# Transformer block in software pipeline: weights in quarters, late constants, and another order of the work at the end

## The chip, the cores and the metric

The program runs on one core of one Trainium2 chip. The metric is the device time of one execution in microseconds (us), median over several runs. Engines are named as the profile names them: PE is TensorE, DVE VectorE, ACT ScalarE, POOL GpSimd, SP the engine that issues most transfers.

## The reference

16 sequences of 256 tokens with 256 features go through two layers; each sequence ("batch" in the kernel) is on its own.

```python
# layer 0: attention of x on the context, 16 heads of 64, then Wo, bo, residual, layer norm
q, k, v = x @ Wq + bq, ctx @ Wk + bk, ctx @ Wv + bv          # 256 -> 1024
x = norm(softmax(mask(q k^T / 8)) v @ Wo + bo + x) * gamma + beta
# layer 1: self attention, 16 heads of 16, with an integer mask
x = norm(x + attention(x, x, mask) @ o_w + o_b)              # ln1
# cross attention on the context, 16 heads of 16, no mask
x = norm(x + attention(x, ctx) @ co_w + co_b)                # ln2
# feed forward 256 -> 1024 -> 256
x = norm(x + relu(x @ lin1_w + lin1_b) @ lin2_w + lin2_b)    # ln3
```

All data is float32.

## The kernel before

**Streams.** The work on one sequence is cut into five streams, which a software pipeline runs side by side for five successive sequences: x (transposes of input and context, first quarter of q and k), a (the attention of layer 0, called A, its Wo and ln0; also keys and values of the context for layer 1), b (self attention, B, and ln1), c (cross attention, C, and ln2's input), m (projection oc of the cross attention, ln2, feed forward, ln3, store).

**Steps.** A list of steps is written out by hand in `schedule` (L49), and every engine walks the same list and does its own part of each step. The kinds are: S, scores of a pair of heads (PE L591, then the masked copy with its extremes on DVE, L868); X, the exponentials on ACT (L698); R, the reciprocal of the sums on DVE (L879) and the scaling on POOL (L959); T, the transposes of the pair on PE (L608) with one copy each by ACT (L705) and DVE (L884); AV, the product with the values for two pairs (PE L633 or L642). J is a job: a product (PE L472) or transposes (PE L478) and its copy on DVE or ACT; h and hd are the quarters of the first feed forward product, y the second, of which a step H does the first half. LN is a layer norm's scaling on DVE (L844), N a next residual on POOL, DMA and IO are transfers issued by SP. Behind S of a pair come R of the pair before it and T of the one before that (`advance`, L105), so that the pairs form one line through all streams. A job's copy on DVE has two PSUM banks, a job's copy on ACT one.

**Bodies.** `bodies` (L320) gives the lists: four that fill the pipeline (x of 0; x, a; x, a, b; x, a, b, c), a loop of 12 turns with all five streams and 24 pairs, and four that empty it: a 15, b 14, c 13, m 12 (24 pairs), then b 15, c 14, m 13 (16 pairs), c 15, m 14 (8 pairs), and m 15. The steps of the missing streams are left out and the others keep their places in the list.

**B and C through DRAM.** Keys and queries of the 16-feature heads are split into a high and a low part on DVE (L811, L816), saved to DRAM and spread from there over the rows of `k4` and `q4`, in eight transfers each (`save_keys` L375, `spread_keys` L386, `spread_queries` L397). The values of C come back from DRAM as well (`load_values` L366). All of these stand on SP's queue in the order of the list, with their waits before them.

**The start.** SP loads x, the context and Wq, the mask, Wk, Wv (1 MB each, L414), the integer mask, Wo, layer 1's attention weights, the small vectors (L428 to L446) and the feed forward weights. ACT loads bq, bk and bv as columns (L656) under one semaphore, and ACT and DVE wait for all three (L659, L746). At the end of the first body ACT waits for all small vectors (L730), DVE too, and adds three bias rows and makes the integer mask (L748); POOL waits for both ahead of its first step (L911, L912).

Of the kernel before, what the change touches and what calls it, by code (L numbers as in the profile page):

```python
# [16 lines left out]
P = 128  # L17
BATCH, TOK, D = 16, 256, 256
TT, DT = TOK // P, D // P
HEADS = 16  # L20
# [27 lines left out]

def schedule(present, carried):  # L49

# [12 lines left out]
    def emit(items):  # L63
        steps.extend(x for x in items if x[3] in present)
# [35 lines left out]
    emit(head)  # L100
    line = [p[1:] for p in carried]
    ready = len(line)
    waiting = [("AV", name, p // 2 - 1, stream) for name, p, stream in line[:1]]

    def advance(g, jobs):  # L105

        nonlocal waiting
        if max(0, ready - 1) <= g - 1 < len(line):
            steps.append(("R",) + line[g - 1])
        emit(jobs)  # L110
        if 0 <= g - 2 < len(line):
            steps.append(("T",) + line[g - 2])
        if ready <= g < len(line):
            steps.append(("X",) + line[g])
        steps.extend(waiting)
        waiting = []
        if 0 <= g - 2 < len(line):
            name, p, stream = line[g - 2]
            if p % 2:
                waiting = [("AV", name, p // 2, stream)]  # L120

    g = ready
    for i, o in enumerate(order):
        if STREAM[o[0]] in present:
            line.append(step("S", *o)[1:])
            steps.append(step("S", *o))
            advance(g, after[o])
            g += 1
        elif carried and "a" not in present and i < 3:
            advance(g, after[o])  # L130
            if i < 2:
                g += 1
            else:
                line, ready, g = [], 0, 0
        else:
            emit(after[o])
    if not closed:
        for k in range(g, g + 3):
            advance(k, [])
        emit(wo + os + first)  # L140
# [3 lines left out]
class Body:  # L144
# [3 lines left out]
    def __init__(self, x, a, b, c, m, before=None, base=None):  # L148
        self.batches = {"x": x, "a": a, "b": b, "c": c, "m": m}
        self.before = before  # L150
        self.base = base or (before.end if before else (0, 0))
        self.present = {s for s, n in self.batches.items() if n is not None}
# [3 lines left out]
        self.steps = schedule(self.present, carried)  # L156
# [7 lines left out]
    def slot(self, step, ring):  # L164

        _, name, p, stream = step
        if stream == STREAM[name]:
            return (self.base[0] + self.pairs.index(("S", name, p, stream))) % ring
        return (self.base[0] - len(self.before.pairs) + self.before.pairs.index(("S", name, p, STREAM[name]))) % ring

    def earlier(self, step, back, same):
# [10 lines left out]
        if len(self.present) == 5:  # L182
# [799 lines left out]
```

## Time and profile before

| | us |
|---|---|
| median of three runs | 2088.13 (2084.88 to 2092.41) |
| profiled execution | 2080.84 |
| its span, first to last instruction | 2079.1 |
| PE busy in the span | 1893.7 (91%) |
| DVE, ACT, POOL busy | 1326.9, 1196.1, 984.2 |
| mean granted clock of PE | 0.970 of full |

Matmuls overlap, so PE's busy time is the time in which at least one was under way. A matmul step's cost is read best from start to start. The granted clock of a stretch is a mean over its two levels.

### The profile page before, as it was taken

To read this page: it belongs to the slowest core of one execution; us is meant where nothing else is said; L and a number is where in the kernel's file an instruction comes from. 1 tells how busy PE (TensorE), PEld (TensorE's weight loads), DVE (VectorE), ACT (ScalarE), POOL (GpSimd) and SP (SyncE) were. 2 spreads that over 40 slices of the span, in tenths; PEclk is the share of its full clock that TensorE was granted. 3 is DMA by queue.
4 is the path that set the end of the run, shared out by engine and by line. 5 is a ranking of instruction groups with operands and counts; after the bars stand their busy time and mean duration, and the time that the engine had idled before them with its cause. 6 is when DMAs were issued, how large, how long until landed. Compare 5 with 4: busy or idle time off the path is not lost.

```text
span 2079.1 us, 42825 instructions
## 1 busy us (share of the span) xinstructions
PE 1893.7 (91%) x12608; PEld 1451.6 (70%) x12608; DVE 1326.9 (64%) x5194; ACT 1196.1 (58%) x3985; POOL 984.2 (47%) x1014
## 2 busy tenths in 40 slices
PE   3999999999999999999899999999999999986776
PEld 2776777777776777777677777767777777764554
DVE  1465676766767676666767666676766667664642
ACT  1454766556565665656666565666656566663632
POOL 0233555536364553645455464544546464552622
PEclk8999999999999999999999999999999999998988
DMA  7032525171422517143260714326071422507120
GB/s 209 28 61 58 87 64 82 33 118 33 77 43 59 92 33 118 33 73 46 54 97 33 119 32 72 47 54 97 32 118 33 80 39 64 86 21 117 25 42 6
DMA packets 145109, 135.94 MB, mean 65 GB/s; under 512 B 23280, under 2 KB 139760, under 8 KB 144880
## 3 DMA queue, kind: packets, MB, share of 16 engines
q1 hardware_dynamic: 141760, 132.97, 35.6%
q8 instruction: 132, 2.16, 0.5%
q14 instruction: 97, 0.79, 0.2%
q10 hardware_dynamic: 3120, 0.01, 0.1%
HBM read 90.99 MB, written 41.94 MB: 64 GB/s over the span
## 4 chain that ended last, share of the span: by engine, by line
PE 64%; issue 16%; POOL 8%; DVE 7%; SPq 2%; ACT 1%; DMA 1%; POOLq 0%; DVEq 0%; ACTq 0%
PE ps_gd L472 27%; PE ps_t L608 10%; PE ps_ga L472 9%; PE ps_s L591 9%; POOL prob L959 7%; PE ps_av L633 5%; PE ps_av L642 4%; DVE prob L868 2%; PE ps_ga L478 1%; DVE res_ln L826 1%; DVE res_ln L844 1%; DVE stats_ln L829 1%; POOL res_ln L947 1%; ACT k_ctx L685 1%; POOL rstd_ln L924 1%
## 5 line engine op out<-in xcount | busy, mean ns | idle before, releaser
L959 POOL TENSOR_TENSOR prob<-prob,recip 128x512 f32<-128x512 f32 x768 | 788.9, 1048 | 927.3 <-DVE recip L879 926.1
L698 ACT ACTIVATE prob<-prob,ext 128x256 f32<-128x256 f32 x1536 | 757.9, 501 | 23.4 <-DVE ext L868 23.3
L705 ACT ACTIVATE prob_t<-ps_t 128x512 f32<-128x512 f32 x384 | 229.2, 597 | 462.5 <-PE ps_t L608 462.4
L608 PE MATMUL ps_t<-ident,prob 128*128 128x128 f32 x3072 | 416.5, 277 | 38.1 <-POOL prob L959 22.7
L608 PEld LDWEIGHTS ps_t<-ident,prob 128*128 128x128 f32 x3072 | 357.4, 142 | 92.6 <-POOL prob L959 31.8
L884 DVE COPY prob_t<-ps_t 128x512 f32<-128x512 f32 x384 | 262.5, 684 | 174.7 <-PE ps_t L608 170.5
L698 ACT ACTIVATION_READ_ACCUMULATOR prob<-prob,ext 128x1 f32 x1536 | 296.9, 193 | 0.0
L868 DVE CUSTOM_DVE_ANT_0 prob<-ps_s,mask_a 128x256 f32<-128x256 f32 x512 | 186.7, 421 | 111.3 <-PE ps_s L591 108.2
L868 DVE CUSTOM_DVE_ANT_0 prob<-ps_s,mask_b 128x256 f32<-128x256 f32 x512 | 187.5, 419 | 73.9 <-PE ps_s L591 73.8
L868 DVE CUSTOM_DVE_ANT_0 prob<-ps_s,zero 128x256 f32<-128x256 f32 x512 | 185.7, 419 | 34.9 <-PE ps_s L591 34.7
L591 PE MATMUL ps_s<-k_ctx,q 64*128 64x256 f32 x1024 | 150.4, 413 | 24.8 <-DVE ext L868 16.2
L685 ACT ACTIVATE k_ctx<-ps_ga,col_bk 128x256 f32<-128x256 f32 x128 | 53.8, 471 | 157.2 <-PE ps_ga L472 140.4
L591 PEld LDWEIGHTS ps_s<-k_ctx,q 64*128 64x128 f32 x1024 | 91.3, 190 | 69.0 <-issue 56.0
L472 PE MATMUL ps_gd<-x_t,wq 128*128 128x256 f32 x512 | 126.6, 391 | 10.2 <-DVE x_t L775 10.2
L472 PE MATMUL ps_ga<-c_t,wk 128*128 128x256 f32 x512 | 127.4, 392 | 0.0
L868 DVE DVE_READ_ACCUMULATOR2_ANT ext<- 128x1 f32 x1536 | 126.9, 83 | 0.0
L633 PE MATMUL ps_av<-prob_t,v 128*64 128x256 f32 x1024 | 124.6, 385 | 0.8 <-DVE prob_t L884 0.8
L472 PE MATMUL ps_gd<-wv,c_t 128*128 128x256 f32 x512 | 124.5, 386 | 0.0
L472 PE MATMUL ps_gd<-wl,h_t 128*128 128x256 f32 x512 | 119.8, 388 | 3.7 <-issue 3.7
L826 DVE TENSOR_TENSOR res_ln<-ps_gd,res_ln 128x512 f32<-128x512 f32 x64 | 44.3, 692 | 122.9 <-PE ps_gd L472 122.9
L844 DVE TENSOR_SCALAR res_ln<-res_ln,mv_ln,rstd_ln 128x256 f32<-128x256 f32 x128 | 82.8, 689 | 62.5 <-issue 54.3
L472 PE MATMUL ps_gd<-wo,k_ctx 128*128 128x256 f32 x512 | 117.2, 382 | 1.0 <-issue 1.0
(87 smaller groups left out, 2567.4 us busy)
## 6 DMA issues: line engine op xcount, KB each, us to landing
k_B<-k_parts_B SPq DMA_DIRECT2D x128, 128.0 KB, 5.2
q_B<-q_parts_B SPq DMA_DIRECT2D x128, 128.0 KB, 9.7
k_C<-k_parts_C SPq DMA_DIRECT2D x128, 128.0 KB, 4.4
q_C<-q_parts_C SPq DMA_DIRECT2D x128, 128.0 KB, 4.8
k_parts_C<-k_hl SPq DMA_DIRECT2D x16, 512.0 KB, 3.0
k_parts_B<-k_hl SPq DMA_DIRECT2D x16, 512.0 KB, 3.4
q_parts_B<-q_hl SPq DMA_DIRECT2D x32, 256.0 KB, 2.4
q_parts_C<-q_hl SPq DMA_DIRECT2D x32, 256.0 KB, 11.5
```

Source lines behind the costliest of these rows:

```text
L472: last = nc.tensor.matmul(out, lhs[i], rhs[i], start=i == 0, stop=i == n - 1)
L591: last = nc.tensor.matmul(two(ps_s[e])[:, t, :], q[r, t * P:(t + 1) * P], k[r], start=True, stop=True)
L608: last = nc.tensor.transpose(two(ps_t[e])[:, kt, qt * P:(qt + 1) * P], src[:, e, qt, kt * P:(kt + 1) * P], ident[:, :])
L633: last = nc.tensor.matmul(two(ps_av)[e * DH0:(e + 1) * DH0, j, :], v0[:, kt, h * DH0:(h + 1) * DH0], pt[:, e, kt, :], start=kt == 0, stop= ...
L642: last = nc.tensor.matmul(ps_av[j * SLOT:(j + 1) * SLOT, 0:TOK], v1[s][:, kt, c:c + SLOT], pt[:, e, kt, :], start=kt == 0, stop=kt == TT - ...
L685: last = nc.scalar.activation(out[:, c, :], ps[:, m, :], ACT.Relu if name == "h" else ACT.Identity, bias=bias[:, c:c + 1])
L698: last = nc.scalar.activation(tile, tile, ACT.Exp, bias=ext[:, slot, e, t:t + 1], scale=-1.0, accum_out=sums[:, slot, e, t:t + 1])
L705: nc.scalar.activation(prob_t[:, body.slot(step, PT_RING), 0], two(ps_t[0]), ACT.Copy).then_inc(pt_act[s], 1)
L844: last = nc.vector.tensor_scalar(y[:, t, :], y[:, t, :], mv[ln][:, t, 0:1], rstd[ln][:, t:t + 1], ALU.subtract, ALU.mult)
L868: last = nc.vector.tensor_tensor_reduce(out=prob[:, slot, e, t, :], in0=two(ps_s[e])[:, t, :], in1=mask, scale=-SCALE[s], scalar=BIG, op0= ...
L884: nc.vector.tensor_copy(prob_t[:, body.slot(step, PT_RING), 1], two(ps_t[1])).then_inc(pt_dve[s], 1)
L959: nc.gpsimd.tensor_tensor(rows, rows, recip[:, slot, e].unsqueeze(2) .to_broadcast([P, TT, TOK]), ALU.mult).then_inc(normed[s], 1)
```

## The change

At the start each of Wq, Wk and Wv is loaded in four pieces of 256 columns, all first quarters ahead of all second ones, each with a semaphore of its own; the row of bo moves up behind the first quarters. ACT and DVE wait for bq and bk alone, and ACT for bv at the first weighed values. The waits for the small vectors, with the bias rows and the integer mask, move from the end of the first body to the end of the second on ACT, DVE and POOL.

At the end the four bodies that empty the pipeline become one, with a list of its own. Sequences 13, 14 and 15 appear in it under the stream names c, c2, c3 and m2, m3, m4. Its 48 pairs come in the order A of 15, B of 14, C of 13, B of 15, C of 14, C of 15; C of 15 uses the buffers `k4`, `q4` and `v1` of B. The three feed forwards stand between the pairs. Before, the first 24 of these pairs were interleaved. The lists of the filling bodies and of the loop have the same steps as before.

```diff
+LAST = {"a": 1, "b": 2, "b2": 1, "c": 3, "c2": 2, "c3": 1, "m": 4, "m2": 3, "m3": 2, "m4": 1}
+HOME = {"c3": "B"}
...
+def last_schedule(carried):
+    steps += [dma("c", "k", "C"), ln("c", "ln1"), job("b", "x1T"), job("a", "mask")]
+    places = [
+        ("A", "a", [
+            [job("b", "ks"), dma("b", "save", "B"), job("a", "k", 1)],
+            [job("b", "qs"), dma("b", "q", "B"), job("a", "q", 1), job("c", "x2T")],
+            [job("c", "qc"), dma("c", "q", "C"), job("a", "v", 0)],
+            [job("a", "k", 2), job("a", "q", 2), io("c", "value_c")],
+            [job("m", "oc"), job("b", "vs")],
+            [ln("m", "ln2"), job("a", "k", 3), job("a", "q", 3)],
+            [job("m", "x3T"), job("a", "v", 1), job("a", "v", 2), res("m", "res3", 0)],
+            [job("a", "v", 3), res("m", "res3", 1)]]),
+        ("B", "b", [
+            [job("m", "h", 0), res("c", "res2", 0)],
+            [job("m", "h", 1), res("c", "res2", 1)],
+            [job("a", "kc"), res("b", "res1", 0)],
+            [half("a", "wo"), res("b", "res1", 1), res("a", "res0", 0)],
+            [job("a", "wo"), job("a", "vc"), io("a", "save_c")],
+            [ln("a", "ln0"), job("m", "hd")],
+            [job("b2", "x1T"), job("m", "h", 2)],
+            [job("b2", "ks"), dma("b2", "save", "B"), job("b2", "qs"), dma("b2", "q", "B")]]),
+        ("C", "c", [
+            [],
+            [half("m", "y")],
+            [job("m", "y")],
+            [job("b", "os"), job("b2", "vs")],
+            [ln("c2", "ln1"), ln("m", "ln3"), io("m", "store")],
+            [job("c2", "x2T")],
+            [job("c2", "qc")],
+            [dma("c2", "k", "C"), dma("c2", "q", "C")]]),
+        ("B", "b2", [
+            [],
+            [],
+            [],
+            [job("m2", "oc"), io("c2", "value_c")],
+            [ln("m2", "ln2")],
+            [job("m2", "x3T"), res("m2", "res3", 0)],
+            [res("m2", "res3", 1)],
+            [dma("c3", "k", "C"), res("c2", "res2", 0)]]),
+        ("C", "c2", [
+            [res("c2", "res2", 1)],
+            [job("m2", "hd"), res("b2", "res1", 0)],
+            [res("b2", "res1", 1)],
+            [job("b2", "os")],
+            [ln("c3", "ln1"), job("m2", "h", 0)],
+            [job("c3", "x2T")],
+            [job("c3", "qc"), dma("c3", "q", "C"), io("c3", "value_c")],
+            [job("m2", "h", 1)]]),
+        ("C", "c3", [
+            [],
+            [],
+            [ln("m2", "ln3"), io("m2", "store")],
+            [job("m3", "oc")],
+            [ln("m3", "ln2")],
+            [job("m3", "x3T"), res("m3", "res3", 0)],
+            [job("m3", "h", 0), res("m3", "res3", 1)],
+            [job("m3", "h", 1), res("c3", "res2", 0)]])]
+    for name, stream, jobs in places:
+        for p in range(PAIRS):
+            if stream == "c3" and p == 0:
+                steps += [job("m2", "h", 2), half("m2", "y"), job("m2", "y")]
+            steps.append(("S", name, p, stream))
+            line.pairs.append(steps[-1][1:])
+            line.advance(g, jobs[p])
+            g += 1
+    line.advance(g, [job("m3", "h", 2), res("c3", "res2", 1)])
+    line.advance(g + 1, [job("m3", "hd")])
+    line.advance(g + 2, [])
+    steps += [job("m4", "oc"), half("m3", "y"), ln("m4", "ln2"), job("m3", "y"), job("m4", "x3T"), ln("m3", "ln3"),
+              io("m3", "store"), job("m4", "h", 0), job("m4", "hd"), res("m4", "res3", 0), res("m4", "res3", 1),
+              job("m4", "h", 1), job("m4", "h", 2), half("m4", "y"), job("m4", "y"), ln("m4", "ln3"), io("m4", "store")]
...
-            body = Body(BATCH - 1, BATCH - 2, BATCH - 3, BATCH - 4, BATCH - 5,
-                        Body(BATCH - 2, BATCH - 3, BATCH - 4, BATCH - 5, None), body.end)
-            for n in range(4):
-                body = Body(*[None] * (n + 1), *range(BATCH - 1, BATCH - 5 + n, -1), body)
-                yield body
+            late = Body({"x": BATCH - 1, "a": BATCH - 2, "b": BATCH - 3, "c": BATCH - 4})
+            yield Body({s: BATCH - n for s, n in LAST.items()}, late, body.end)
...
-            def spread_keys(s, b):
+            def spread_keys(s, b, home):
                 sp.wait_ge(k_saved[s], count(b, 16, 16))
-                if s == "C" and not (isinstance(b, int) and b == 0):
+                if s != home:
+                    sp.wait_ge(scored["B"], count(b, HEADS, HEADS))
+                elif s == "C" and not (isinstance(b, int) and b == 0):
                     sp.wait_ge(scored["C"], count(b - 1, HEADS, HEADS))
...
-            for w, n in ((wq0, "q0"), (wk0, "k0"), (wv0, "v0")):
-                sp.dma_start(w[:, :, :], wide(L0 + "W" + n[0])).then_inc(w_in[n], 16)
-                if n == "q0":
-                    sp.dma_start(mask_u8[:, :, :], m_d[:, 0]).then_inc(m_in, 16)
+            for i in range(4):
+                cols = slice(i * D, (i + 1) * D)
+                for w, n in ((wq0, "q"), (wk0, "k"), (wv0, "v")):
+                    sp.dma_start(w[:, :, cols], wide(L0 + "W" + n)[:, :, cols]).then_inc(w_in0[n][i], 16)
+                    if i == 0 and n == "q":
+                        sp.dma_start(mask_u8[:, :, :], m_d[:, 0]).then_inc(m_in, 16)
+                if i == 0:
+                    sp.dma_start(row["bo0"][:, :], io[L0 + "bo"].partition_broadcast(P)).then_inc(w_in["bo0"], 16)
...
-                        pe.wait_ge(w_in[name + "0"], 16)
+                        pe.wait_ge(w_in0[name][i], 16)
...
-                              ).then_inc(w_in["bias0"], 16)
-            act.wait_ge(w_in["bias0"], 48)
+                              ).then_inc(w_in["bias_v" if n == "bv" else "bias0"], 16)
+            act.wait_ge(w_in["bias0"], 32)
...
-            dve.wait_ge(w_in["bias0"], 48)
+            dve.wait_ge(w_in["bias0"], 32)
...
-                if body.before is None and body.batches["x"] is not None:
+                if body.present == {"x", "a"}:
                     constants_of_layer1()
...
-            pool.wait_ge(w_in["small"], 16 * small)
-            pool.wait_ge(dve_const, 2)
+            pool.wait_ge(w_in["bo0"], 16)
+            pool.wait_ge(dve_const, 1)
...
+                if body.present == {"x", "a"}:
+                    pool.wait_ge(w_in["small"], 16 * small)
+                    pool.wait_ge(dve_const, 2)
```

## Rows read from the trace of the kernel before

**Rows 1.** Stretches of single bodies (us, busy of PE, PEld, DVE, ACT, POOL, PEclk, DMA, GB/s)

```profile
1515.05:1633.48 118.43, 115.04 (x788) 89.03 (x788) 81.11 (x321) 72.75 (x243) 60.33 (x62) 1.00 0.36 65
1753.59:1874.36 120.77, 113.63 (x767) 86.88 (x765) 81.70 (x322) 73.77 (x248) 61.99 (x64) 0.97 0.37 61
1874.36:1970.82 96.46, 68.07 (x447) 48.80 (x445) 54.08 (x218) 48.38 (x162) 42.96 (x45) 0.86 0.44 66
1970.82:2034.75 63.93, 44.12 (x249) 31.04 (x249) 30.62 (x118) 27.53 (x91) 23.45 (x27) 0.84 0.27 43
2034.75:2079.10 44.35, 26.92 (x124) 19.61 (x124) 9.15 (x22) 5.62 (x13) 7.24 (x9) 0.79 0.02 6
```

**Rows 2.** Timeline of the start, all engines (start us, duration, instruction, idle before it)

```profile
16.21 0.69 DVE L775 COPY x_t<-ps_gd 128x512 f32<-128x512 f32 x1 [14.46 <-DMA col_bv<-L_xattn_bv]
...
25.77 1.98 PE L591 MATMUL ps_s<-k_ctx,q 64*128 64x256 f32 x8 [2.36 <-ACT k_ctx L685]
...
27.68 2.79 PE L472 MATMUL ps_ga<-c_t,wk 128*128 128x256 f32 x8
...
42.44 1.09 DVE L751 TENSOR_TENSOR row_b<-row_b,h_t 128x256 f32<-128x256 f32 x3 [20.95 <-DMA h_t<-L_xattn_lin_b]
...
45.98 2.08 PE L591 MATMUL ps_s<-k_ctx,q 64*128 64x256 f32 x8 [15.51 <-DVE ext L868]
```

**Rows 3.** DMA issues of the first 60 us (KB each, us from issue to landing)

```profile
col_bk<-L_xattn_bk ACTq DMA_DIRECT2D x1, 4.0 KB, 8.5
col_bv<-L_xattn_bv ACTq DMA_DIRECT2D x1, 4.0 KB, 14.2
```

**Rows 4.** Timeline of PE in the last body with A pairs

```profile
1825.06 1.13 PE L591 MATMUL ps_s<-k_ctx,q 64*128 64x256 f32 x8
1826.12 3.72 PE L472 MATMUL ps_gd<-wl,h_t 128*128 128x256 f32 x16
1829.68 1.04 PE L608 MATMUL ps_t<-ident,prob 128*128 128x128 f32 x8
1830.64 0.50 PE L591 MATMUL ps_s<-k_C,q_C 64*128 64x256 f32 x4
```

**Rows 5.** A group of the page's costliest (busy, mean ns of one, idle before)

```profile
L698 ACT ACTIVATE prob<-prob,ext 128x256 f32<-128x256 f32 x1536 | 757.9, 501 | 23.4 <-DVE ext L868 23.3
```

**Rows 6.** Timeline of DVE at a batch's last layer norm

```profile
2014.40 1.44 DVE L844 TENSOR_SCALAR res_ln<-res_ln,mv_ln,rstd_ln 128x256 f32<-128x256 f32 x2
```

**Rows 7.** Three stretches with few jobs, columns as in group 1

```profile
1858.47:1874.36 15.89, 13.13 (x90) 8.61 (x89) 12.15 (x52) 10.57 (x38) 8.89 (x10) 0.79 0.15 28
1920.88:1966.44 45.56, 35.88 (x270) 24.19 (x270) 31.36 (x134) 32.88 (x115) 30.46 (x30) 0.91 0.02 7
2011.02:2034.75 23.73, 15.03 (x106) 9.58 (x105) 18.91 (x77) 15.83 (x54) 12.38 (x14) 0.78 0.04 12
```

**Rows 8.** Timeline of PE, scores of pairs in three light slots

```profile
1942.82 0.80 PE L591 MATMUL ps_s<-k_B,q_B 64*128 64x256 f32 x4 [0.29 <-DVE ext L868]
...
1947.75 0.50 PE L591 MATMUL ps_s<-k_B,q_B 64*128 64x256 f32 x4
...
1953.70 0.51 PE L591 MATMUL ps_s<-k_B,q_B 64*128 64x256 f32 x4
```

**Rows 9.** Timeline of PE, y of batches 14 and 15

```profile
2002.29 8.80 PE L472 MATMUL ps_gd<-wl,h_t 128*128 128x256 f32 x32 [2.69 <-issue]
...
2064.25 7.14 PE L472 MATMUL ps_gd<-wl,h_t 128*128 128x256 f32 x32 [0.98 <-issue]
```

**Rows 10.** Timeline of PE and SP, products and first scores of B and C

```profile
1877.73 1.97 PE L472 MATMUL ps_gd<-x_t,w_k 128*128 128x256 f32 x8 [2.77 <-ACT x_t L677]
...
1904.67 0.80 PE L591 MATMUL ps_s<-k_B,q_B 64*128 64x256 f32 x4 [11.08 <-issue]
...
1978.66 1.29 SPq L400 DMA_DIRECT2D q_parts_C<-q_hl  x2
...
1993.67 0.50 PE L591 MATMUL ps_s<-k_C,q_C 64*128 64x256 f32 x4
```

More of the change, by code:

```diff
@@ L46, with __init__, advance @@
 NEXT = {"a": "b", "b": "c", "c": "m"}
+LAST = {"a": 1, "b": 2, "b2": 1, "c": 3, "c2": 2, "c3": 1, "m": 4, "m2": 3, "m3": 2, "m4": 1}
+HOME = {"c3": "B"}
+class Line:
+    def __init__(self, steps, carried):
+        self.steps = steps
+        self.pairs = [p[1:] for p in carried]
+        self.ready = len(self.pairs)
+        self.waiting = [("AV", name, p // 2 - 1, stream) for name, p, stream in self.pairs[:1]]
+    def advance(self, g, jobs):
+        pairs = self.pairs
+        if max(0, self.ready - 1) <= g - 1 < len(pairs):
+            self.steps.append(("R",) + pairs[g - 1])
+        self.steps.extend(jobs)
+        if 0 <= g - 2 < len(pairs):
+            self.steps.append(("T",) + pairs[g - 2])
+        if self.ready <= g < len(pairs):
+            self.steps.append(("X",) + pairs[g])
+        self.steps.extend(self.waiting)
+        self.waiting = []
+        if 0 <= g - 2 < len(pairs):
+            name, p, stream = pairs[g - 2]
+            if p % 2:
+                self.waiting = [("AV", name, p // 2, stream)]
 def schedule(present, carried):
@@ L61, in schedule, with here @@
     steps = []
-    def emit(items):
-        steps.extend(x for x in items if x[3] in present)
+    def here(items):
+        return [x for x in items if x[3] in present]
     order = [(name, 2 * q + j) for name, q in
@@ L98, in schedule @@
     }
[L100 to L120, printed above, removed]
@@ L122, in schedule @@
-    g = ready
-    for i, o in enumerate(order):
+    steps += here(head)
+    line = Line(steps, carried)
+    g = line.ready
+    for o in order:
         if STREAM[o[0]] in present:
-            line.append(step("S", *o)[1:])
             steps.append(step("S", *o))
-            advance(g, after[o])
+            line.pairs.append(steps[-1][1:])
+            line.advance(g, here(after[o]))
             g += 1
[L129 to L134, printed above, removed]
@@ L248, in program @@
         two = lambda t: t[:, :].rearrange("p (a n) -> p a n", a=2)
-        w_in = {n: sem("w_in_" + n) for n in ("q0", "k0", "v0", "bias0", "out0", "attn1", "mlp", "small", "mask")}
+        w_in = {n: sem("w_in_" + n) for n in ("bias0", "bias_v", "bo0", "out0", "attn1", "mlp", "small", "mask")}
+        w_in0 = {n: [sem(f"w_in_{n}0_{i}") for i in range(4)] for n in "qkv"}
         x_in, c_in, m_in = sem("x_in"), sem("c_in"), sem("m_in")
@@ L259, in program @@
         att = "ABC"
-        small = len(col) - 3 + 2 + len(row) + 3
+        small = len(col) - 3 + 2 + len(row) - 1 + 3
         SPREAD = 8
@@ L340, in load @@
                 b = body.batch(step)
-                if body.batches["a"] is None:
+                if "a" not in body.present:
                     return
@@ L712, in evac_weighed @@
                     act.wait_ge(weighed[s], count(b, QUADS, quad + 1))
+                    if isinstance(b, int) and b == 0:
+                        act.wait_ge(w_in["bias_v"], 16)
                     for j in range(2):
@@ L901, in _ @@
                      "AV": evac_weighed}.get(step[0], lambda *_: None)(body, step)
-                if body.before is None and body.batches["x"] is not None:
+                if body.present == {"x", "a"}:
                     constants_of_layer1()
```

63 lines of the change are left out of this document (40 added, 23 removed).

## The prediction

> **What bounds the kernel now.** I read the page first (busy shares and the 40 slices), then the stretches of single bodies, then the timeline of the first 60 us and of the last 325. In the loop TensorE sets the pace: a body of 118.4 us has it busy 115.0 us at full granted clock [rows 1]. The change leaves the loop's order as it is, so the question is the two ends. In the last body that has A pairs TensorE is still busy 113.6 of 120.8 us; in the three stretches behind it it is busy 68.1 of 96.5, 44.1 of 63.9 and 26.9 of 44.4 us, and the granted clock is 0.86, 0.84 and 0.79 [rows 1]. Together this end takes 120.8 + 96.5 + 63.9 + 44.4 = 325.5 us. In them TensorE idles 72.8 us and runs slow on top. At the start the first tile is copied by VectorE only at 16.21, first scores stand ready at 25.77, and then nothing moves until VectorE adds the bias rows at 42.44; the second scores run at 45.98 [rows 2].
>
> **The head, part by part.** (1) VectorE and ScalarE no longer wait for the column of bv. Its row says 14.2 us to landing, bk's 8.5 [rows 3]; bv landed at 16.2, so was issued at 2.0, and bk just ahead of it, which puts bk at 10 at the latest. It may come sooner, since less is queued in long packets; nothing before 4, when x_tok's transposes start, could use it, and their results are complete at about 7 (an estimate: c_tok comes next on the same queue). I take 8.5 for the first copy, between the bounds 7 and 10. (2) Wq, Wk, Wv come in 12 pieces with the first pieces in front. From first copy to first scores the kernel needs 25.77 - 16.21 = 9.6 us [rows 2] and this stays: 18.1. The later quarters have to be there about one pair apart; all 4 MB of weights up to Wo and more land well before 42 today, so I cost them nothing. If this cover fails, the product of k's quarter 1, which is the next on TensorE, waits. (3) The long wait goes: ScalarE, VectorE and GpSimd wait for the small constants after body 1, which today ends at 107.7 and then at some 85, still over 40 us behind the landing. What is late next is TensorE's own k product: the second scores follow the first by a 2.0 us score step and the 2.8 us product that today hides in the wait [rows 2], so at 22.9, against 45.98: 23.1 gained. (4) The bias sums and the mask, 1.4 us from 42.44 on VectorE, move behind body 1, where body 2's first scores wait for them: 1.4 back. [...] With no 16 us hole before it I give 1 us for that and the q product behind it. (6) Nine more DMAs on SP's queue, each around 0.5 us of issue, push all later loads by 5 us, which nothing waits for. Bounds of these: 19 to 26; taken 22.7, say **23 us**.
>
> **The end.** Nothing is removed: the same 48 pairs and jobs stand in another order, so I price slots. A slot is what lies between two score steps. On TensorE the steps cost, start to start, 1.06 (A's scores), 0.44 (B's and C's, 0.50 long), 0.97 (turning a pair), 1.8 (a product of eight matmuls: half of 3.56), 3.56 (half of y or wo), 1.0 (weighing B or C) and 1.9 (A) [rows 4]. ScalarE needs 4 exponentials of 0.50 us and a copy [rows 5], 2.6, VectorE four reductions, two reciprocals and a copy, some 2.3, GpSimd two products, some 2.1. A layer norm adds 1.44 on VectorE [rows 6]; for the last one of a batch, which multiplies and adds a row behind it, I count 3.6, two more passes. A slot's price is its largest engine's sum. For the last A body this rule gives 120.5, where 120.8 were measured [rows 1]. For slots with few jobs it falls short: 13.3 against 15.9, 40.6 against 45.6 and 19.6 against 23.7 [rows 7], 16% in sum, since a pair's chain and a clock of 0.78 to 0.91 come in. Two empty slots take 5.95 us together [rows 8], where ScalarE has some 5.7.
> The new order, step by step:
> - 20 full slots (all of A, of B of batch 14, the first four of C of 13), 6.7 us for a slot with two products, less towards the end: 112 by the rule, plus 3 because x1T and h2, and h after h, now share one bank of ScalarE with nothing but a turn between. 115.
> - 26 light slots (C 13's last four, B 15, seven of C 14, seven of C 15), 99.2 by the rule, 3.8 each, since residuals, norms and projections are spread over them; times 1.16: 115.
> - The slot of C 14's last pair, which holds h1, h2 and all of y: 12.2, and 2.7 for the wait before y that the same series had at 2002.29 [rows 9]: 15.
> - From C 15's last scores to the turn of its pair 6: 3.4 today, with h1 and h2 in it 6.
> - The rest, 44.4 us today. Batch 14's hd and y (8.9 us of TensorE) now fill the waits around the last projection, where TensorE has only 26.9 us of work in 44.4 [rows 1]. By steps: turn, weigh, hd, turn, weigh 7.2 with two short waits; oc 1.8; y 7.1; x3T and its copy 1.8; h0, hd, h1 5.3; h2 with a wait 2.8; a wait of 1 and y 7.1, and from y's end to the end 2079.1 - 2071.4 = 7.7 [rows 9]: 42.
> Sum 293, against 325.5: **32 us** gained. Round trips through DRAM: for B of 15 TensorE stood idle for 11.1 us until 1904.67, 27 us after its key product began [rows 10]. Now the product stands over 30 us ahead of its first score, behind C's eight pairs: hidden. For C of 15 the save starts at 1978.66 and the scores ran at 1993.67 [rows 10], so 15.0 us are enough; the new order has 17 us of TensorE work between. It is the tightest one. C 14's keys can only be spread after C 13's last scores, with eight B pairs, 27 us, for it. If they fail, the exposed part adds in full.
> SP's queue stays in order: the store of batch 12 waits for its norm ahead of C 14's spread, but that waits for C 13's last scores anyway, some 10 us later.
> **Sum:** 23 + 32 = 55. The span goes from 2079.1 to 2024 and the profiled execution (2080.84, below all three timed runs) to 2026. The median shown is 7.3 higher, 2088.13, and I put the gain on that: 2033. What measurement can tell from no change is about 0.3%, 6 us.
>
> **Rivals.**
> R1, the pairs' own pace. The light slots run as the rule says or as the empty ones do, 2.98 [rows 8], because jobs fill the clock's holes: 99 instead of 115, and the drain two better. For: a clock of 1.00 where TensorE is kept busy [rows 1]. Against: all three light stretches were 12 to 21% above the rule. With a head of 25, gain 75: 2013.
> R2, low clock at the end. [...] At the lower level a slot without jobs took 4.9, from 1942.82 to 1947.75 [rows 8]. If half of the 26 slots do so, 13 times 1.2 is 16 us, and with a head of 20 the gain is 36: 2052. Against: small products stand in most slots.
> [...]
> R3, the quarters come late. Loads of 1 KB rows in place of 4 KB ones bind the first pairs, and the first A attention runs at the pace of the transfers: half the head's gain, 11, is lost: 2044. Against: bv's column, queued beside x, c and over a megabyte of weights, was in at 16.2 [rows 3], and the 12 pieces are wanted over more than 30 us, k's second at 20.
> R4, slower: the round trips open up. In the new order three attentions wait on a spread (B 15, C 14, C 15) with no pair of another kind behind them in the hand-written order. If SP's in-order queue held each as B 15 was held today, 27 us from the key product [rows 10], and the pairs between did not cover it, 81 us would be added: 2033 + 81 = 2114. It decides when the uncovered part is over 18 us for each. Against: eight pairs, at least 24 us, stand ahead of each.
> R5, the change does not bite, as bk or a late constant still holds the start and the end's slots lose what they gain: under 6 us either way.
>
> **Numbers.** Forecast 0.60, R1 0.12, R2 0.18, R3 0.06, R4 0.02, R5 0.02. Faster takes the first four, 0.96; same 0.01 and slower 0.03 share the rest. The range goes to R1 and R2: 2013 to 2053.
>
> **What would show it.** First copy by VectorE at 7 to 10; second scores at 22 to 24; no engine waiting for a bias row; second body's start near 86. The part behind the loop near 293 us, TensorE's idle time in it 35 to 45 instead of 73, no idle over 3 us before a first score of B 15, C 14 or C 15, and the last product ending 7.7 before the end. Wrong would be: a wait on Wk's quarter before 30, any spread that shows as idle time, granted clock under 0.85 in the light stretch, or light slots of over 4.8 us.

## The result and the profile after

The changed kernel takes 2005.18 us in the median of four runs (2000.32 to 2012.25), the kernel before 2086.51 beside it on the same chip (2083.13 to 2092.41): a ratio of 0.961, 95% interval 0.9573 to 0.9647. The forecast was 2033, with 2013 to 2053. The sign was right and the size was not: 81 us were gained where 55 were forecast, and the range's lower bound lies 8 us above the result. The profiled execution took 2005.85 us, its span is 2004.1, against 2079.1. Two executions further down, one of `head_only` (2101.76 us) and one of `h2_moved` (6322.16 us), ran in a slower state and are left out of the medians and ratios given there.

First the stretches of the changed kernel, columns as in [rows 1]. In order: one loop body; the end in five parts (20 full slots, 19 light slots, the slot of C 14's last pair with h1, h2 and y, 7 light slots, the rest); the whole end; the loop.

```profile
1486.85:1606.59 119.74, 116.58 (x788) 90.05 (x788) 81.24 (x321) 72.67 (x243) 60.27 (x62) 0.99 0.37 63
1730.01:1845.26 115.25, 109.62 (x714) 85.73 (x712) 74.24 (x284) 64.01 (x213) 54.66 (x58) 0.99 0.54 85
1845.26:1914.66 69.40, 56.71 (x449) 39.50 (x448) 57.82 (x241) 54.95 (x188) 48.50 (x49) 0.93 0.41 62
1914.66:1928.30 13.64, 12.37 (x64) 10.11 (x60) 3.47 (x14) 5.24 (x19) 2.07 (x3) 1.00 0.86 136
1928.30:1956.81 28.51, 22.20 (x169) 15.19 (x168) 23.90 (x94) 18.91 (x64) 16.57 (x18) 0.88 0.03 10
1956.81:2004.10 47.29, 34.91 (x196) 28.27 (x192) 16.77 (x46) 10.70 (x31) 13.96 (x17) 0.95 0.04 12
1730.01:2004.10 274.09, 235.81 (x1582) 178.81 (x1580) 176.21 (x678) 153.81 (x511) 135.77 (x142) 0.95 0.38 61
270.51:1730.01 1459.50, 1394.44 (x9459) 1077.96 (x9457) 992.97 (x3889) 894.07 (x2989) 738.17 (x757) 0.99 0.37 65
```

The end fell from 325.5 to 274.1 us. TensorE idles 274.09 - 235.81 = 38.3 us in it, before 72.8 [rows 1]; the other 17 us of the gain are busy time, for the most part the same matmuls at a higher clock, 0.95 in the mean where the last three stretches before had 0.79 to 0.86. This is a split of the time and not yet the price of the clock: in `filled_light2` below the light slots have a clock of 0.98 and 1.00 in place of 0.93 and 0.88 and take 97.2 us for 97.9. `filled_old_end` measures the price in the old end.

Two things in reading such rows. Busy time of TensorE is less than the sum of its matmuls: in the kernel before the 512 with Wo take 382 ns each in the mean, 195.6 us together, and are counted as 117.2 us busy. Steps overlap too: the first three of [rows 4] take 1.13 + 3.72 + 1.04 = 5.89 us, and from the start of the first to the start of the fourth it is 5.58. And in all fourteen traces the record of the granted clock has two values, 1.00 and 0.50, the lower one most often for 3.41 us at a time (15 of the changed kernel's 17 pieces); 0.93 or 0.88 is a mean over both.

Next the start, on the timeline, to be read against [rows 2], and the landings of bk and bv against [rows 3].

```profile
6.86 0.69 DVE L880 COPY x_t<-ps_gd 128x512 f32<-128x512 f32 x1 [5.11 <-DMA col_bk<-L_xattn_bk]
...
7.65 3.75 PE L574 MATMUL ps_gd<-x_t,wq 128*128 128x256 f32 x8 [1.20 <-DVE x_t L880]
...
14.04 1.28 ACT L788 ACT_TABLE_LOAD   x1 [14.04 <-PE ps_ga L574]
...
16.32 2.08 PE L694 MATMUL ps_s<-k_ctx,q 64*128 64x256 f32 x8 [2.37 <-ACT k_ctx L788]
18.33 2.69 PE L574 MATMUL ps_ga<-c_t,wk 128*128 128x256 f32 x8
...
20.95 1.13 PE L694 MATMUL ps_s<-k_ctx,q 64*128 64x256 f32 x8
```

```profile
col_bk<-L_xattn_bk ACTq DMA_DIRECT2D x1, 4.0 KB, 5.5
col_bv<-L_xattn_bv ACTq DMA_DIRECT2D x1, 4.0 KB, 8.2
```

The 16 us hole in front of the second scores is gone: they run at 20.95 in place of 45.98. Bodies are counted from 0 here, as the prediction does: body 0 has x of sequence 0 alone, body 1 the first attention A, body 2 the first B. What the prediction and the expectations call the second body is body 2. It starts at 81.88, before at 108.64. Seven of the traces here have this same start, and body 2 starts in them at 79.6 to 82.2; in the earliest, `mixed_first`, the granted clock up to there was 1.00, here 0.98. What a single edit of the start gives can be told only above these 2.5 us. The rest of the start is a chain without a gap to spare: bk's landing, the copies, q's product (3.75 us for eight matmuls that take 1.99 at 22.02), k's (2.76), and ScalarE's table load of 1.28 ahead of the first keys. The changed kernel's stretches of q's product, the first and the second scores:

```profile
7.65:11.40 3.75, 3.75 (x9) 3.03 (x10) 0.50 (x1) 0.00 (x0) 0.00 (x0) 1.00 1.12 328
16.32:18.40 2.08, 2.08 (x9) 1.38 (x9) 0.00 (x0) 0.00 (x0) 0.00 (x0) 0.51 1.10 350
20.95:22.08 1.13, 1.13 (x10) 0.75 (x9) 0.00 (x0) 1.02 (x3) 0.00 (x0) 1.00 1.13 302
```

The same scores take 2.08 us at 0.51 and 1.13 at 1.00. For q's product no low clock is shown: the record begins at 12.9 us, and stretches ahead of that read 1.00. That it ran at the lower level is an estimate, from its 3.75 us against 1.99.

Span against span: 26.8 us from the start, 51.4 from the end, and 3.2 given back in the loop, whose code is the same: 75.0. The median moved by 81.3, because the profiled execution before (2080.84) was lower than all the runs beside it.

What TensorE waited for in the end, as groups of waits (us in total, times, longest). The changed kernel:

```profile
PE ps_t L711 <- POOL prob L1064: 5.2, 10, 1.1
PE ps_s L694 <- DVE ext L973: 4.1, 7, 0.9
PE ps_t L711 <- DVE prob_t L989: 3.5, 4, 1.6
...
PE ps_ga L580 <- DVE res_ln L949: 3.3, 3, 1.7
PE ps_ga L574 <- ACT x_t L780: 3.2, 2, 2.0
```

And the old end, from the first experiment below, where it stands behind the new start:

```profile
PE ps_s L724 <- issue: 12.6, 2, 10.4
PE ps_t L741 <- POOL prob L1094: 10.0, 18, 1.8
PE ps_s L724 <- DVE ext L1003: 9.9, 13, 1.9
PE ps_ga L610 <- DVE res_ln L979: 7.7, 2, 3.8
PE ps_gd L604 <- ACT x_t L810: 7.2, 5, 2.8
```

The round trip of B 15 (the 10.4 us before its first scores, put down to "issue" since nothing in the profile releases it) has no row any more, and the waits on a pair's own chain (its scaling on GpSimd, its extremes and copies on VectorE) and on the jobs' copies are about halved.

### The profile page after: what moved, and what is told of

It reads as the page before. It is cut to its first block, busy times and chain, and to the rows that moved or that the text cites. A ratio compares the mean times of both kernels' runs of the same rounds, so it can differ in the third digit from the quotient of the medians.

```text
span 2004.1 us, 42839 instructions
## 1 busy us (share of the span) xinstructions
PE 1876.5 (94%) x12608; PEld 1443.8 (72%) x12608; DVE 1327.3 (66%) x5194; ACT 1194.2 (60%) x3985; POOL 984.2 (49%) x1014
## 4 chain that ended last, share of the span: by engine, by line
PE 64%; issue 18%; POOL 9%; DVE 5%; ACT 2%; DMA 0%; POOLq 0%; DVEq 0%; ACTq 0%
PE ps_gd L574 27%; PE ps_t L711 10%; PE ps_ga L574 9%; PE ps_s L694 9%; POOL prob L1064 7%; PE ps_av L736 5%; PE ps_av L745 4%; DVE prob L973 2%; PE ps_ga L580 1%; DVE res_ln L931 1%; POOL res_ln L1052 1%; ACT k_ctx L788 1%; DVE stats_ln L934 1%; DVE res_ln L949 1%; ACT prob L801 0%
## 5 line engine op out<-in xcount | busy, mean ns | idle before, releaser
L949 DVE TENSOR_SCALAR res_ln<-res_ln,mv_ln,rstd_ln 128x256 f32<-128x256 f32 x128 | 84.4, 701 | 63.3 <-issue 56.7
L574 PE MATMUL ps_gd<-wo,k_ctx 128*128 128x256 f32 x512 | 117.2, 382 | 1.7 <-issue 1.0
```

The lines of the kernel that those rows point to most:

```text
L574: last = nc.tensor.matmul(out, lhs[i], rhs[i], start=i == 0, stop=i == n - 1)
L949: last = nc.vector.tensor_scalar(y[:, t, :], y[:, t, :], mv[ln][:, t, 0:1], rstd[ln][:, t:t + 1], ALU.subtract, ALU.mult)
```

## The experiments

Twelve kernels ran, in three groups, each beside the kernel before (2085.14, 2086.44 and 2085.0 us in the median). Where no interval is given there was one run. Of the edits only the lines that matter are shown.

**The two halves apart.** `head_only` has the new start and the four old emptying bodies:

```
-            late = Body({"x": BATCH - 1, "a": BATCH - 2, "b": BATCH - 3, "c": BATCH - 4})
-            yield Body({s: BATCH - n for s, n in LAST.items()}, late, body.end)
+            late = Body({"x": BATCH - 2, "a": BATCH - 3, "b": BATCH - 4, "c": BATCH - 5})
+            body = Body(dict(zip("xabcm", range(BATCH - 1, BATCH - 6, -1))), late, body.end)
+            for n in range(4):
+                body = Body(dict(zip("abcm"[n:], range(BATCH - 1, BATCH - 5 + n, -1))), body)
+                yield body
```

> The changed start with the four emptying bodies of before. If the two ends are independent: second body's first TensorE work at 82 us as in the changed kernel (108.7 before), part behind the loop 325 us as before, time 27 us under before, a ratio of 0.987. Rival, that the loop or the end gives part of it back: ratio over 0.990, with the part behind the loop or a loop body longer than before.

2059.59 us, ratio 0.986 (0.9822 to 0.9898). Body 2 starts at 82.16. The part behind the loop takes 324.2 us, as four bodies (columns as above):

```profile
1734.04:1853.74 119.70, 112.28 (x766) 86.06 (x765) 81.72 (x322) 73.77 (x248) 61.58 (x64) 0.99 0.37 60
1853.74:1951.29 97.55, 68.39 (x446) 48.74 (x445) 54.09 (x218) 48.48 (x162) 43.37 (x45) 0.86 0.44 66
1951.29:2015.44 64.15, 44.28 (x248) 31.05 (x248) 30.63 (x118) 27.53 (x91) 23.61 (x27) 0.84 0.28 43
2015.44:2058.22 42.78, 25.31 (x124) 18.50 (x124) 9.15 (x22) 5.62 (x13) 7.26 (x9) 0.84 0.02 7
```

`end_only` is the reverse: weights whole, all three biases waited for, constants in the first body, and the new end.

> The start of before with the new single body at the end. If the end's gain is its own: part behind the loop 274 us, 51 less than before, ratio 0.975, and the two parts add up to the whole change within 5 us. Rival, that the end is helped by the earlier start (transfers, clock): part behind the loop over 280.

2036.63 us, ratio 0.9764 (0.9737 to 0.9791). The part behind the loop takes 274.5 us, body 2 starts at 109.14. The halves are independent: in the traces the new start alone brings body 2 forward by 26.5 us and the new end alone is 51.0 shorter, against 26.8 and 51.4 together. The medians give 25.6 + 48.5 = 74 us of the 81, within what medians of a few runs tell.

**Is it the clock?** The light slots fell short of the forecast's price, and the clock in them was 0.93 and 0.88, not 0.78 to 0.91. `filled_light2` is the changed kernel with transposes of the identity wherever TensorE waits in the light slots; they write to PSUM that is overwritten right after:

```
+                    if light:
+                        busy(body, step, two(ps_t[e])[:, 0, 0:P], 2)
+                    pe.wait_ge(normed[s], count(b, HEADS, 2 * p + e + 1))
```

> The changed kernel with extra transposes of the identity, whose results are overwritten, where TensorE waits in the light slots: 2 ahead of each half of a turn, 4 to 14 ahead of oc and the transposes of x2 and x3. The output stays the same. If the low clock after a wait is what the light slots still lose: granted clock 0.93 and 0.88 there go to about 1.00 and the 26 light slots from 97.9 to about 91 us. Rival, that VectorE, ScalarE and GpSimd set them: clock up, time the same or longer by up to 5 us, as the extra work stands in the way.

2004.86 us, ratio 0.9611 (0.9585 to 0.9638): no change. Its two light stretches:

```profile
1843.58:1913.60 70.02, 64.41 (x543) 47.58 (x542) 58.90 (x242) 55.12 (x190) 48.50 (x49) 0.98 0.42 64
1927.24:1954.38 27.14, 24.59 (x217) 18.19 (x216) 23.81 (x94) 19.17 (x66) 17.04 (x19) 1.00 0.03 10
```

The clock is at 0.98 and 1.00 now, and the slots take 97.2 us against 97.9. The added transposes could have cost as much as the clock gave, so a comparison without them counts more: six traces have the changed kernel's end as it is. In the changed kernel TensorE had the low clock for 17.1 us of the light slots and they took 97.9 us, in the five others (`end_only`, `warm_head`, `whole_weights`, `bv_waited`, `const_early`) for 13.7 us and they took 98.4. In the full slots, where TensorE is busy 95%, it does count: `const_early` had no low clock there and took 113.6 us, the others 3.4 us of it and 115.2. `filled_old_end` asks the same of the old end: `head_only` with such transposes in the three bodies without an A, 70 of them in front of B 15's first scores.

> The new start with the old end (four bodies that empty in turn), and identity transposes on TensorE where its steps wait in the three emptying bodies without a last-layer A, 70 of them ahead of B15's first scores, so that the engine hardly rests there. Theory (the low clock made an own part of the old end's time, so whole attentions win partly by keeping the clock): the part behind the loop falls from 324 to 305-312 us, about 2045. Rival (the gaps are waits for other engines and for the round trip, the low clock lies inside them): 322-328 us, the time stays at 2060 +/- 4.

2054.09 us, ratio 0.9845 (0.9823 to 0.9868), the part behind the loop 321.5 us:

```profile
1732.44:1856.16 123.72, 116.15 (x770) 88.59 (x769) 82.20 (x324) 74.24 (x249) 61.93 (x64) 0.96 0.35 59
1856.16:1954.07 97.91, 86.94 (x660) 70.03 (x659) 54.29 (x217) 48.22 (x162) 43.27 (x45) 0.97 0.43 66
1954.07:2013.06 58.99, 49.46 (x344) 38.27 (x342) 30.53 (x117) 27.01 (x91) 23.23 (x26) 0.94 0.29 46
2013.06:2053.95 40.89, 28.95 (x190) 23.46 (x190) 9.15 (x22) 5.83 (x14) 7.25 (x9) 0.95 0.02 7
```

The clock rises from 0.84 to 0.94 and 0.95, and the three filled bodies lose 97.55 + 64.15 + 42.78 - 97.91 - 58.99 - 40.89 = 6.7 us; the first, where nothing was changed, was 4.0 longer this time. So of the 51 us of the new end some 7 can be the clock, or more if the added transposes stood in the way themselves, which was not measured. The run fell short of its theory (305 to 312 us). The first of the three, the one with the round trip, gained nothing from it.

**Is it the whole attentions, or only one body without drains?** `mixed_first` keeps one body, but its first 24 pairs stand interleaved as in the loop (AAABCBACBBCC by twos), and only B 15, C 14 and C 15 follow as whole attentions:

```
+    order = [(name, 2 * q + j) for name, q in
+             zip("AAABCBACBBCC", (0, 1, 2, 0, 0, 1, 3, 1, 2, 3, 2, 3)) for j in range(2)]
```

> One body at the end as in the change, but its first 24 pairs interleaved A, B, C as before, with Wo's layer norm late; B 15, C 14, C 15 then follow. If doing A as a whole first is what hides the round trip of B 15 through DRAM: TensorE idles 12 to 20 us ahead of B 15's first scores and the part behind the loop takes 288 to 297 us. Rival, that having one body with no drain between is the gain: that part stays within 5 us of 274.

2009.27 us, ratio 0.9633 (0.9606 to 0.966), the part behind the loop 278.4. The first 24 pairs and B 15's first scores:

```profile
1727.91:1864.59 136.68, 116.19 (x796) 90.28 (x794) 86.95 (x334) 76.87 (x258) 63.23 (x66) 0.96 0.47 76
```

```profile
1864.59 0.80 PE L695 MATMUL ps_s<-k_B,q_B 64*128 64x256 f32 x4 [13.68 <-issue]
```

The interleaved order does its 24 pairs in 136.7 - 13.7 = 123.0 us, the changed kernel in 1863.17 - 1730.01 = 133.2. It saves 10, some 2 of them because the transposes of x2 and the product qc of C 14 stand behind B 15's first scores in it, and pays 14 for B 15's round trip, which now has nothing in front of it. So whole attentions among the first 24 pairs bring 4 of the 51 us, by covering that one trip; the other 47 come with the single body. It has two parts, a line of pairs that doesn't run dry between the streams, and norms, projections and feed forwards placed between other pairs; no run tells them apart.

**The head's three parts.** One is undone in each of the next three. `whole_weights`, each weight in one transfer:

```
-            for i in range(4):
+            for i in range(1):
```

> The changed kernel with each first-layer weight loaded by one transfer again, the rest of the new start kept. Theory (the quarters bring the small constants and the first weight forward, part of the head's gain): the first copy on ScalarE at 8 to 9 in place of 6.86, the first scores at 17.5 to 19 in place of 16.32, 1 to 3 us of the 27. Rival (the first projections wait for whatever lands last anyway): first scores within 0.5 of 16.32.

2005.08 us. The first copy waits for bk until 8.69, the first scores run at 17.21; but k's product takes 1.89 us, above 2.76, and the first scores 1.14 at a granted clock of 1.00, above 2.08 at 0.51; the second scores run at 20.20 and body 2 starts at 81.03. The first scores, 0.9 later, fall between theory and rival. A start 1.8 us later is given back within five steps: nothing is left. `bv_waited`, on ScalarE and VectorE alike:

```
-            act.wait_ge(w_in["bias0"], 32)
+            act.wait_ge(w_in["bias0"], 48)
```

> The changed kernel, but ScalarE and VectorE wait for the value bias together with the two other biases before their first step, as the kernel before does. Theory: the first copy waits for the third bias, at 10 to 14, and the first scores come 3 to 7 us later than 16.32. Rival (with the quarters the value bias lands close behind the others): first scores at most 1.5 us later.

2010.01 us. First copy at 10.34, first scores at 18.75, 2.4 later, but body 2 at 82.57, 0.7 later. Of the 4.2 us by which its span is longer 2.7 lie in the loop and 0.4 in the end, which this edit does not touch. The copy came as the theory had it, the first scores between theory (3 to 7 later) and rival (at most 1.5); for body 2 it is under 1 us, less than the same start varies by. `const_early`, on all three engines:

```
-                if body.present == {"x", "a"}:
+                if body.present == {"x"}:
```

> The changed kernel with the late constants back in the first body. Theory (they hold ScalarE and VectorE ahead of the second scores, the largest term of the head): second scores at 40 to 47 in place of 20.95, body 2 18 to 24 us later than 81.88, about 2025. Rival (body 1 has slack that takes the delay up): body 2 under 10 us later.

2039.7 us, body 2 at 111.48, 29.6 later, above the 18 to 24 expected. Its timeline, VectorE's bias rows and TensorE's second scores:

```profile
44.44 1.10 DVE L856 TENSOR_TENSOR row_b<-row_b,h_t 128x256 f32<-128x256 f32 x3 [32.31 <-DMA h_t<-L_xattn_lin_b]
```

```profile
47.98 2.08 PE L694 MATMUL ps_s<-k_ctx,q 64*128 64x256 f32 x8 [26.80 <-DVE ext L973]
```

This is the whole head, and more: with twelve weight pieces ahead of them on SP's queue the constants land 2 us later than before (44.44 against 42.44 in [rows 2]). The late constants are worth 29.6 us, the quarters and the bias of v nothing that can be told; without the late constants the new start would have lost 2 to 3 (111.48 against 109.14 in `end_only`).

**What is left at three places.** `warm_head` puts identity transposes on TensorE at the very start, behind the context's transposes and behind k's first product, and has ScalarE load its table by a small activation at the beginning.

> The changed kernel with identity transposes on TensorE before and between the first steps, and ScalarE's table loaded by a small activation at the very start. Theory (the first projections run at the low or just raised clock and the 1.28 us table load stands in the chain from the keys to the first scores): first scores at 12.5-14 in place of 16.32, body 2 some 3 us earlier, 2002. Rival (the chain is set by landings and by the copies on ScalarE and VectorE): first scores 15.5-16.5, 2005.

2000.5 us, ratio 0.9602 (0.9574 to 0.963). TensorE's first steps:

```profile
1.43 1.97 PE L754 MATMUL ps_av<-ident 128*128 128x128 f32 x8 [1.43 <-POOL ident L1024]
...
8.08 1.97 PE L575 MATMUL ps_gd<-x_t,wq 128*128 128x256 f32 x8 [0.54 <-DVE x_t L890]
...
12.86 1.13 PE L695 MATMUL ps_s<-k_ctx,q 64*128 64x256 f32 x8 [0.43 <-ACT k_ctx L798]
```

First scores at 12.86, body 2 at 76.79, 5.1 earlier. Here the matmuls' own pace does count: q's and k's products take 1.97 and 1.89 us in place of 3.75 and 2.76, and the first scores 1.13 at a granted clock of 1.00 in place of 2.08 at 0.51. The table load left the chain too: from the end of k's product to the first scores it is 1.1 us, before 2.4, so it is 1.3 of the 3.5 us at the first scores. The 5.1 are the best case: against the changed start at its luckiest (79.6) it is 2.9, and in `tuned`, with the same start as here, body 2 came at 80.0.

`h2_moved` takes h2 from the slot of B 14's pair 6, where it waits for ScalarE's copy of x1T (the idle time in this row of the changed kernel), and puts it into that of C 13's pair 0:

```profile
1815.10 3.68 PE L574 MATMUL ps_ga<-x_t,wl 128*128 128x256 f32 x8 [2.03 <-ACT x_t L780]
```

```
-            [job("b2", "x1T"), job("m", "h", 2)],
+            [job("b2", "x1T")],
```

> The changed kernel with the h2 step of c1 put one slot block later (from the slot of B6's last pair, where x1T of b2 uses the same bank, to C0's). Theory (slot B6 took 8.67 us against 4.81 by the rule since h2 waits 2.03 us for ScalarE's copy of x1T): B6 falls to about 5, C0 grows by under 1, 3 us gained, 2002. Rival (the slots share what the engines owe, as in the light stretch as a whole, 97.9 against 99.2): the stretch of light slots keeps 97-99 us and the time 2005 +/- 2.

1997.02 us, ratio 0.9594 (0.9558 to 0.963), the part behind the loop 270.7. The slots from B's pair 6 to C's pair 3, first the changed kernel, then this one:

```profile
1811.91:1845.26 33.35, 30.13 (x197) 23.33 (x196) 22.25 (x88) 17.32 (x60) 14.89 (x18) 0.95 0.62 96
```

```profile
1806.46:1835.70 29.24, 28.23 (x197) 22.25 (x196) 22.08 (x88) 17.32 (x60) 14.89 (x18) 1.00 0.73 109
```

4.1 us, 1.9 of them matmuls at a higher clock: in this execution a wait of 2 us cost nearly as much again through the clock of the product behind it (3.68 us at 0.54, 1.99 at 1.00 in `h2_moved`). It need not: in `const_early`, behind the same wait of 2.03 us, that product took 1.99 us at 1.00.

`split_ln3` gives the last norm's scaling, gain and bias slots of their own. In the changed kernel they keep VectorE in one piece, while a pair's transposed probabilities wait for their copy:

```profile
1847.61 2.87 DVE L949 TENSOR_SCALAR res_ln<-res_ln,mv_ln,rstd_ln 128x256 f32<-128x256 f32 x4
1850.51 0.69 DVE L956 TENSOR_TENSOR res_ln<-res_ln,row_g 128x512 f32<-128x512 f32 x1
1851.23 0.69 DVE L958 TENSOR_TENSOR res_ln<-res_ln,row_b 128x512 f32<-128x512 f32 x1
1851.84 0.68 DVE L989 COPY prob_t<-ps_t 128x512 f32<-128x512 f32 x1
```

> The changed kernel with the last layer norm's VectorE work (3.6 us in one piece) as three steps in slots of their own. Theory (one long piece on VectorE holds back the copies of the transposed probabilities: C5 and C6 take 6.28 and 6.86 us against 3.62 and 4.58): those slots fall, 3 to 5 us gained, about 2001. Rival (a slot before took less than its rule, so the stretch is bound by the sums of the engines' work and not by its pieces): light slots 97-99 us as before, 2005 +/- 2.

1999.93 us, ratio 0.9587 (0.9567 to 0.9607), the part behind the loop 270.8. Its light stretches:

```profile
1845.19:1913.88 68.69, 56.09 (x449) 38.43 (x448) 58.64 (x241) 55.09 (x188) 49.61 (x49) 0.93 0.41 62
1927.52:1953.48 25.96, 19.17 (x169) 13.23 (x168) 23.62 (x94) 18.92 (x64) 17.46 (x18) 1.00 0.03 11
```

94.65 us against 97.91, with VectorE as busy as before (82.3 against 81.7 us). Of the 3.3 us 0.7 lie in the first stretch and 2.6 in the second. Filling the waits gave nothing in these slots, cutting up what is waited for did. In the slot shown the edit also takes apart two norms that stood together (the scaling x4 is of both), so there the cutting isn't told from the moving; in the second stretch the norm stood alone.

`tuned` has these three edits together.

> The changed kernel with the three edits that each gave something: identity transposes and the table load at the start (body 2 came 5.1 us earlier), h2 out of slot B6 (the part behind the loop 3.4 us shorter), the last norm in three pieces (3.3 us shorter). Theory (they touch different places and add): body 2 at 77, the part behind the loop 266 to 269, 1990 to 1996 us. Rival (h2 moved and the split norm relieve the same VectorE queue): the part behind the loop 270 to 272, 1998.

2000.58 us in five runs (1997.05 to 2003.72), ratio 0.9588 (0.9564 to 0.9612), above the 1990 to 1996 expected. The end adds up as expected, 266.7 us, 7.4 shorter; body 2 came at 80.00, not 77, since q's product took 3.75 us again in this execution; and the loop took 3.5 us more. By spans it is 5.3 us below the changed kernel, by ratios 0.9588 against 0.961 with intervals that overlap, and it is level with each single edit. Faster than the kernel before it surely is; than the changed one probably, by some 0.2%.

## Why the prediction fell short, step by step

**Bounds now** was right: the loop is TensorE's (busy 1394.4 of 1459.5 us), the change acts at both ends only, and these add up.

**Head, (1).** bk was taken to allow the first copy at 8.5, between 7 and 10. It was 6.86, below the lower bound, and 8.69 with the weights whole: the quarters, which the sum priced at nothing, bring bk forward. First scores 16.32 for 18.1.

**(2)** right: no product waits for a quarter. **(3)** right, and the largest term: second scores at 20.95 for 22.9, the difference being (1). **(4)** was given 1.4 us and cost nothing: no engine was late behind body 1. Body 2 follows after the same 0.9 us as in every kernel here with either place of the constants (80.95 to 81.88; 110.55 to 111.48 in `const_early`), and from its start to the loop it is 188.6 us, before too. **The 1 us for the second scores and the q product behind them**: no run shows this term. From the second to the third scores the kernel before takes 5.66 us (45.98 to 51.64), the changed one 3.84 (20.95 to 24.79), 1.8 less. The second scores take 2.08 us at a granted clock of 0.50 before and 1.13 at 1.00 now, the q product 2.88 and 1.99. The head gave 26.8 against 22.7, over its upper bound of 26 (26.5 to 29.0 over the seven traces with this start). The reasoning that the constants carry it was right; `whole_weights` and `bv_waited` show that the other two parts, on which (1) and (2) rest, are worth next to nothing on their own: of a start 1.8 or 3.5 us later all or most was given back, in one trace each, k's product taking 1.89 us in both in place of 2.76 and the first scores 1.14 and 1.13 at a granted clock of 1.00 in place of 2.08 at 0.51.

**End.** Of the five terms three stand to within 2 us: the 20 full slots 115.25 for 115, the slot with y 13.6 for 15 (the wait before y was 1.2, not 2.7), and C 15's last scores with the rest 47.3 for 48. The term that failed is the second: **26 light slots, 99.2 by the rule, times 1.16: 115**. They took 69.40 + 28.51 = 97.9. The bare rule was right in sum, and this is R1's price for them, which had 0.12.

The factor came from three stretches of before [rows 7] and was carried to slots that are not of their kind. In `head_only` nine slots of C 14 and B 15, seven of them empty and two with a norm, took 33.65 us where the rule has about 28, a fifth more; in `filled_old_end`, at a clock of 0.95 for 0.85, the same nine took 31.24. So there are two parts: the clock, and the pair's own chain, 5.95 us for two empty slots [rows 8], where the rule has some 5.4. In the new order the list gives only six of the 26 nothing beside their pair; they took 18.06 us for the rule's 16 to 17. The other twenty carry a norm, a residual or a product and took 79.9 for 82 to 83, less than the rule. There a slot's largest engine is VectorE with a norm or GpSimd with a residual, and their excess lies partly beside the next slot's TensorE work: a largest sum for each slot counts it in full. A factor on top went the wrong way. That both parts were at work in the nine slots is shown; why the twenty stay under the rule is only argued.

**R1** was nearest in time (2013) and right for the light slots; its gain of 75 is the gain of the span, 75.0, though part of that is luck: the head gave 2 and the rest of the end 1 more than it had, and the loop took 3. Its reason, that jobs fill the clock's holes, was not right: filling the holes altogether (`filled_light2`) changed nothing. **R2** had 0.18. Taken together the light slots of the changed kernel are not bound by the clock; in the old end its own share is some 7 us. The clock does fall in the light slots of the changed kernel, to 0.93 and 0.88 against 0.99 in the full ones. A low clock had a price at the start (2.08 us for the first scores at 0.51, 1.13 at 1.00 in `warm_head`) and in the slot of h2 (3.68 us for the product at 0.54, 1.99 at 1.00). In the light slots it came to nothing: TensorE is busy 56.7 of 69.4 us and 22.2 of 28.5 there and waits for another engine anyway. **R3** did not come: with the weights whole body 1 takes 62.9 us from its first scores, in quarters 64.6, the clock being 1.00 and 0.97, and no product waits for a piece. **R4** did not come either: the changed kernel shows no wait over 3 us before any attention's first scores; but its mechanism is real, 13.7 us for B 15 in `mixed_first`, where its cover is gone. **R5** is out.

**Numbers.** Of the 28 us between 2033 and 2005, 4 are the head and 19 the end (17 of them light slots), and the loop took 3 back. The other 8 are the median on which the gain was put: it lay 7.3 us over the profiled execution before, and after the two agree within 0.7. So the forecast failed by the factor 1.16, and the range by its base: its lower bound was R1, which has the light slots right and the gain of 75 that the span shows. The 8 us by which the result lies under that bound are this base.

## What to carry to other kernels

Price a reordered stretch by each slot's largest engine, and correct it only with slots that carry the same mix of jobs: an excess measured on empty slots belongs to the chain of an empty slot (here a fifth in nine nearly empty slots, and none in twenty with jobs). In a pipeline's end first remove the places where it runs dry (here, with the feed forwards spread between the pairs, 47 us), then see that each round trip through memory has a whole attention in front of it (here 4). Before a transfer at the start is split finely, look for the wait behind which everything stands: here the one for the small constants was worth 30 us, and the finer transfers nothing that could be told.

## What the runs showed of the hardware

The loop is the same code in all these kernels, and it took 1454.1 to 1463.5 us. The trace's record of the granted clock accounts for most of it. Added up over the loop, the time at the lower level, 0.50, was 20.5 us in `warm_head`, 30.7 in the changed kernel and 37.5 in `tuned` and `head_only`. The loop's time less half of that is 1443.9, 1444.1, 1444.2 and 1444.1 us, and between 1442.7 and 1446.4 in all fourteen traces, that of the kernel before among them (1456.3 less half of 27.3). The loop's rows in `warm_head` and in `tuned` show it too:

```profile
265.89:1719.99 1454.10, 1389.26 (x9458) 1074.55 (x9457) 992.80 (x3889) 894.19 (x2989) 738.26 (x757) 0.99 0.39 65
```

```profile
269.13:1732.14 1463.01, 1397.70 (x9458) 1080.17 (x9457) 993.32 (x3889) 894.58 (x2989) 739.05 (x757) 0.99 0.38 65
```

The other engines' busy times agree within 1 us, TensorE's differs by 8.4 of the 8.9 us: the same matmuls, with 17 us more of the time at 0.50 (37.5 against 20.5), half of which is 8.5. The low clock falls now on one product and now on another, also here, where TensorE is busy 95.5% of the time: in six pieces of 3.41 us in `warm_head`, the first 243 us behind the loop's start, in nine in the changed kernel and eleven in `tuned`, the first 87 us behind it in both. No edit of the loop was there to steer it. The swing of 9 us is more than any of the last edits gave: each of these was read from its own stretch, and by total times they can't be ranked. The stretches swing too where their code is unchanged, by 2.5 us for the start, 1.7 for the full slots and 0.5 for the light ones. The 3.4 and 3.3 us of `h2_moved` and `split_ln3` stand clear of that, the gain of `warm_head` hardly.
